# Attention, group norm and ternary feed-forward in one kernel: the inverse softmax sums of two heads travel through DRAM instead of over TensorE

## What is computed

```
s1 = q1 @ k1^T * scale + causal mask ; a1 = softmax(s1)      # 16 heads, q1, q2, k1, k2 of 32 columns each, with rope
s2 = q2 @ k2^T * scale + causal mask ; a2 = softmax(s2)
out = (a1 - lam * a2) @ v                                    # v has 64 columns, 4 key-value heads
out = (out - mean(T, 64)) * rsqrt(var(T, 64) + eps) * gn_w + gn_b       # over time and width of one head
x = layernorm(x + (out * KEEP) @ Wo)
x = layernorm(x + down(silu(up(x)) * gate(x)))               # weights quantised to -1, 0, 1 times a scale
```

## Time and profile before

| what | value |
|---|---|
| median of 3 runs | 2199.38 us (2192.79 to 2201.3) |
| profiled execution: its own time | 2201.01 us |
| profiled execution: span from first to last instruction | 2196.6 us |
| granted TensorE clock, mean over the span | 0.992 |
| PE busy, share of the span | 97% |
| DVE busy | 77% |
| ACT busy | 66% |
| POOL busy | 54% |
| bytes moved by DMA | 263.85 MB, mean 120 GB/s |

### The profile page before, as it was taken

The page is one execution under the profiler, slowest core; times in us unless marked ns, Lnnn a source line. Parts: engine busy times, 40 slices in busy tenths (PEclk is TensorE's granted clock), DMA queues, the critical chain, the costliest instruction groups (busy, mean ns, idle before and its releaser), DMA issues.

```text
span 2196.6 us, 41181 instructions
## 1 busy us (share of the span) xinstructions
PE 2125.6 (97%) x13314; PEld 1367.8 (62%) x13314; DVE 1688.4 (77%) x3701; ACT 1458.0 (66%) x3450; POOL 1194.4 (54%) x1919
## 2 busy tenths in 40 slices
PE   8999999999999999999999999999999999999998
PEld 4666666666665766666666666666666666654443
DVE  4888888889888887788887888878778788853333
ACT  0777777667776777777667777777677687742232
POOL 0577666677655655555654655655455555531232
PEclk9999999999999999999999999999999999999999
DMA  7666576757655512212462322342552212114000
GB/s 252 200 210 219 195 216 198 238 180 221 189 163 149 163 51 61 92 50 62 145 153 79 97 68 84 96 125 73 154 116 54 73 40 87 49 49 110 6 20 19
DMA packets 291217, 263.85 MB, mean 120 GB/s; under 512 B 65088, under 2 KB 233152, under 8 KB 288960
## 3 DMA queue, kind: packets, MB, share of 16 engines
q1 hardware_dynamic: 279808, 228.65, 35.6%
q10 hardware_dynamic: 11200, 32.58, 4.6%
HBM read 181.48 MB, written 71.30 MB: 115 GB/s over the span
## 4 chain that ended last, share of the span: by engine, by line
PE 77%; DVE 8%; POOL 5%; issue 5%; ACT 4%; DMA 1%; ACTq 0%; DVEq 0%; SPq 0%; POOLq 0%
PE PS L1171 18%; PE PS L1120 11%; PE PS L1101 10%; PE PS L1082 10%; PE PS L1140 9%; PE PS L1161 9%; PE PS L1180 8%; PE PS L1147 2%; DVE e_long L1458 2%; POOL linv L1383 2%; ACT dt_long L1222 1%; ACT e_long L1232 1%; POOL coef L1384 1%; PE PS L1086 1%; DVE e_long L1524 1%
## 5 line engine op out<-in xcount | busy, mean ns | idle before, releaser
L1383 POOL TENSOR_TENSOR linv<-lsum,powers 128x2 f32<-128x2 f32 x512 | 405.7, 792 | 415.5 <-ACT e_long L1232 340.2
L1232 ACT ACTIVATE e_long<-e_long,nmax 128x768 f32<-128x768 f32 (+3 forms) x512 | 505.2, 987 | 159.5 <-DVE nmax L1458 156.8
L1458 DVE CUSTOM_DVE_ANT_0 e_long<-PS,mask_b 128x768 f32<-128x768 f32 (+3 forms) x512 | 516.8, 1019 | 82.1 <-PE PS L1101 61.0
L1101 PE MATMUL PS<-kstk,qstk 128*128 128x384 f32 (+5 forms) x1536 | 479.0, 416 | 19.6 <-DVE nmax L1458 9.5
L1101 PEld LDWEIGHTS PS<-kstk,qstk 128*128 128x128 f32 x1536 | 269.7, 191 | 144.5 <-issue 83.8
L1222 ACT ACTIVATE dt_long<-PS 128x512 f32<-128x512 f32 (+3 forms) x544 | 258.4, 514 | 136.5 <-PE PS L1082 126.5
L1524 DVE SCALAR_TENSOR_TENSOR e_long<-e_long,coef 128x1024 f32<-128x1024 f32 (+3 forms) x256 | 276.6, 1080 | 68.4 <-POOL coef L1384 68.0
L1232 ACT ACTIVATE e_short<-e_short,nmax 128x384 f32<-128x384 f32 (+3 forms) x512 | 283.1, 557 | 20.1 <-DVE nmax L1458 19.4
L1396 POOL TENSOR_TENSOR hid<-th,hid 128x512 f16<-128x512 f32 x128 | 148.2, 1160 | 248.8 <-ACT hid L1272 129.6
L1384 POOL TENSOR_SCALAR coef<-lsum,linv,neglam 128x1 f32<-128x1 f32 x512 | 233.2, 456 | 53.4
L1082 PE MATMUL PS<-ident,e_long 128*128 128x128 f32 x1664 | 239.6, 276 | 13.9 <-DVE nmax L1458 7.1
(11 more groups left out here) (117 smaller groups left out, 3114.9 us busy)
## 6 DMA issues: line engine op xcount, KB each, us to landing
qstk<-dq SPq DMA_DIRECT2D x512, 128.0 KB, 2.9
dq<-hl SPq DMA_DIRECT2D x25, 1024.0 KB, 5.1
wr<-in_w_proj ACTq DMA_DIRECT2D x48, 512.0 KB, 5.1
kstk<-dk SPq DMA_DIRECT2D x64, 256.0 KB, 5.2
da<-ra SPq DMA_DIRECT2D x32, 512.0 KB, 3.3
at_sb<-da SPq DMA_DIRECT2D x32, 512.0 KB, 4.3
wt<-in_w_up SPq DMA_DIRECT2D x16, 512.0 KB, 6.0
wt<-in_w_gate SPq DMA_DIRECT2D x16, 512.0 KB, 5.5
```

The costliest lines, as they stand in the source:

```text
L1101: last = nc.tensor.matmul(slot[:, h, :], qstk[:, duo % 4, 2 * r + m, :].bitcast(F32R), kstk[:, g % 2, m, h * w:(h + 1) * w].bitcast(F32R), ...
L1232: nc.scalar.activation(e, e, ACT.Exp, bias=nmax[:, u % 8:u % 8 + 1], scale=-1.0, accum_out=lsum[:, n % 4, m:m + 1]).then_inc(s_exp, 1)
L1383: link(nc.gpsimd.tensor_tensor(linv[:, a % 8, :], lsum[:, a % 4, :], mone, ALU.pow))
L1458: nc.vector.tensor_tensor_reduce(out, slot, mask, -1.0, -NEG, ALU.add, ALU.min, nmax[:, u % 8:u % 8 + 1]).then_inc(s_negmax, 1)
```

## The change

The way of the inverses is another one. `spread`, turn and copy are gone: POOL no longer writes `wide`, PE no longer turns it, ACT evicts only key blocks, and `r_short` and the last block of `dt_long` are gone. Instead SP issues, for each duo, one store of the two columns of `linv` (128 partitions, two numbers of 4 bytes each) to two rows of 128 numbers in DRAM (`dinv`), waits for its landing, and issues two loads, each of which reads one row into 64 partitions of a new tile `inverses` (four duos deep). `product` waits for the rows and multiplies by them. The eviction of a head step no longer waits for the product that read the rows out of the same tile. `factor` waits, from head step 8 on, for the landing of the store that last read its column of `linv`. In the planner the new DMAs get costs (0.5 and 0.9 us on SP) and a landing time of 3.0 us each, evictions and turns get the costs of their key blocks alone, and `PACE` goes from 3.75 to 3.6.

```diff
@@ -63,14 +63,9 @@
-def in_line(duo):
-    return STEPS[heads_of(duo)[0]].t != 3
-    return (STEPS[n].t + STEPS[n].r) // 4 + 1
+    return STEPS[n].t // 4 + 1
@@ -206,7 +201,7 @@
-LANDS = {"load q": 4.5, "load k": 7.5, "load v": 6.0, "store v": 7.0, "store rotated": 8, "store a": 4.5, "load a": 6.5,
+LANDS = {"store inverses": 3.0, "load inverses": 3.0, "load q": 4.5, "load k": 7.5, "load v": 6.0, "store v": 7.0, "store rotated": 8, "store a": 4.5, "load a": 6.5,
@@ -216,8 +211,7 @@
-    t, r = STEPS[n].t, STEPS[n].r
-    return min(4, t + 1 + r - 4 * half), min(4, t + 1 - 4 * half)
+    return min(4, STEPS[n].t + 1 - 4 * half)
@@ -233,7 +227,7 @@
-        return 0.109 * blocks_of(a, b)[0] + 0.02
+        return 0.109 * blocks_of(a, b) + 0.02
@@ -241,10 +235,7 @@
-        blocks, keys = blocks_of(a, b)
-        if in_line(STEPS[a].duo) or blocks == keys:
-            return 0.06 + 0.107 * blocks
-        return 0.22 + (0.06 + 0.107 * keys if keys else 0)
+        return 0.06 + 0.107 * blocks_of(a, b)
@@ -253,11 +244,11 @@
-        return 1.4 if STEPS[a].r else 1.15
+        return 1.15
-            "load q": 1.0, "load k": 1.9, "load first": 0.5, "load x1": 0.5, "load wo": 0.48, "load a": 0.5, "store v": 0.45,
+            "store inverses": 0.5, "load inverses": 0.9, "load q": 1.0, "load k": 1.9, "load first": 0.5, "load x1": 0.5, "load wo": 0.48, "load a": 0.5, "store v": 0.45,
@@ -296,10 +287,6 @@
-            if STEPS[back].r:
-                out.append(ITEM("product", STEPS[back].duo))
-        if STEPS[a].r and not in_line(STEPS[a].duo) and STEPS[a].duo >= 8:
-            out.append(ITEM("product", STEPS[a].duo - 8))
@@ -371,7 +358,7 @@
-        out = [ITEM("values", run_of(a))]
+        out = [ITEM("values", run_of(a)), ITEM("load inverses", a)]
@@ -390,9 +377,12 @@
-        if STEPS[a].r and STEPS[a].duo >= 2:
-            second = heads_of(STEPS[a].duo - 2)[1]
-            out.append(ITEM("turn", second, turns(second) - 1))
+        if a >= 8:
+            out.append(ITEM("store inverses", STEPS[a - 8].duo))
+    elif what == "store inverses":
+        out = [ITEM("factor", heads_of(a)[1])] + [ITEM("load inverses", a - 4)] * (a >= 4)
+    elif what == "load inverses":
+        out = [ITEM("store inverses", a)] + [ITEM("product", a - 4)] * (a >= 4)
@@ -476,6 +466,7 @@
+           [ITEM("store inverses", duo) for duo in range(DUOS)], [ITEM("load inverses", duo) for duo in range(DUOS)],
@@ -487,9 +478,9 @@
-         "sum": -1.5, "ternary": -1.5, "side": -1.0, "rsqrt": 1.0, "product": 0.5, "load q": 2.0, "store rotated": 3.0}
+         "sum": -1.5, "ternary": -1.5, "side": -1.0, "rsqrt": 1.0, "product": 0.5, "load q": 2.0, "store inverses": 1.5, "load inverses": 1.5, "store rotated": 3.0}
-PACE = 3.75
+PACE = 3.6
@@ -697,6 +688,7 @@
+    dinv = nc.dram_tensor("dinv", (DUOS, 2, P), F32, kind="Internal").ap()
@@ -745,10 +737,9 @@
-        dt_long = [sb(f"dt_long{r}", [P, NT + r, P]) for r in range(2)]
+        dt_long = [sb(f"dt_long{r}", [P, NT, P]) for r in range(2)]
-        r_short = sb("r_short", [P, P])
-        wide = sb("wide", [P, 2, 2, 64])
+        inverses = sb("inverses", [P, 4, P])
@@ -845,7 +836,8 @@
-        s_wide = sem("s_wide")
+        s_inv = [sem(f"s_inv{k}") for k in range(4)]
+        s_rows = [sem(f"s_rows{k}") for k in range(4)]
@@ -870,6 +862,9 @@
+        def inverses_stored(eng, duo):
+            eng.wait_ge(s_inv[duo % 4], 16 * (duo // 4 + 1))
@@ -958,6 +953,21 @@
+            def store_inverses(duo):
+                second = heads_of(duo)[1]
+                sp.wait_ge(s_coef, second + 1)
+                sp.dma_start(dinv[duo].rearrange("r q -> q r"), linv[:, (second - 2) % 8:second % 8 + 1:2, 0],
+                             allow_slow_non_contiguous=True)\
+                    .then_inc(s_inv[duo % 4], 16)
+            def load_inverses(duo):
+                inverses_stored(sp, duo)
+                if duo >= 4:
+                    multiplied(sp, duo - 4)
+                for r in range(2):
+                    sp.dma_start(inverses[64 * r:64 * r + 64, duo % 4, :], dinv[duo, r:r + 1, :].broadcast_to((64, P)))\
+                        .then_inc(s_rows[duo % 4], 16)
@@ -1044,6 +1054,10 @@
+                elif what == "store inverses":
+                    store_inverses(a)
+                elif what == "load inverses":
+                    load_inverses(a)
@@ -1076,15 +1090,9 @@
-                blocks, keys = blocks_of(n, half)
-                for k in range(keys):
+                for k in range(blocks_of(n, half)):
-                if blocks > keys:
-                    duo = STEPS[n].duo
-                    pe.wait_ge(s_wide, duo + 1)
-                    last = nc.tensor.transpose(F[bank][:, keys * P:blocks * P],
-                                               wide[:, duo % 2, :, :].rearrange("p r d -> p (r d)"), ident[:, :])
@@ -1206,24 +1214,14 @@
-                blocks, keys = blocks_of(n, half)
-                duo = STEPS[n].duo
+                blocks = blocks_of(n, half)
-                    if STEPS[back].r:
-                        multiplied(act, STEPS[back].duo)
-                if half == 0 and STEPS[n].r and not in_line(duo) and duo >= 8:
-                    multiplied(act, duo - 8)
-                here = blocks if in_line(duo) else keys
-                if here > 0:
-                    copied = nc.scalar.activation(
-                        dt_of(n)[:, 4 * half:4 * half + here, :].rearrange("p k q -> p (k q)"), F[bank][:, 0:here * P], ACT.Copy)
-                if here < blocks:
-                    copied = nc.scalar.activation(r_short[:, :], F[bank][:, here * P:blocks * P], ACT.Copy)
-                copied.then_inc(s_ffree[bank], 1)
+                nc.scalar.activation(dt_of(n)[:, 4 * half:4 * half + blocks, :].rearrange("p k q -> p (k q)"),
+                                     F[bank][:, 0:blocks * P], ACT.Copy).then_inc(s_ffree[bank], 1)
@@ -1378,17 +1376,12 @@
-                    duo = STEPS[a].duo
+                    if a >= 8:
+                        inverses_stored(pool, STEPS[a - 8].duo)
-                    if STEPS[a].r:
-                        if duo >= 2:
-                            second = heads_of(duo - 2)[1]
-                            pool.wait_ge(s_tb, TURN[second, turns(second) - 1] + 1)
-                        nc.gpsimd.tensor_copy(wide[:, duo % 2, :, :], linv[:, (a - 2) % 8:a % 8 + 1:2, 0:1]
-                                              .broadcast_to((P, 2, 64))).then_inc(s_wide, 1)
@@ -1542,12 +1535,13 @@
-                    rows = dt_of(heads_of(a)[1])[:, t + 1, :] if in_line(a) else r_short[:, :]
+                    dve.wait_ge(s_rows[a % 4], 32 * (a // 4 + 1))
-                    nc.vector.tensor_tensor(ra[:, chunk % 2, t * P:(t + 1) * P], F[bank][:, a % 2 * P:a % 2 * P + P], rows,
+                    nc.vector.tensor_tensor(ra[:, chunk % 2, t * P:(t + 1) * P], F[bank][:, a % 2 * P:a % 2 * P + P],
+                                            inverses[:, a % 4, :],
```

## The result

The changed kernel takes 3056.81 us (median of 4 runs, 3038.47 to 3063.27) where the kernel before takes 2197.53 us: 1.390 times the time of before, 95% interval 1.383 to 1.397. The profiled execution took 3038.47 us, with a span of 3036.7 us. The forecast was 2173.4 us, with a range up to 2200.

A forecast was written before the change was run, and what follows sets the result against it. PE was taken to bound all three stages, with DVE close behind in the first. Terms -28.9 - 2 - 2 + 2 + 5 = -26 us gave 2175 us against the profiled execution, 2173.4 us for the median; range 2150 to 2200.

The forecast's parts named there:

- What bounds the kernel: Whole run: PE sets the time in all three stages, busy 97% of the span; taking columns from it shortens the run.
- Turns, POOL, ACT and pace: Attention: fewer turned blocks -28.9 us, lone turns -2, POOL's copies -2, ACT's evictions nothing, closer pace +5.
- The new way of the rows: Store, landing and loads ahead of DVE's product: path 5.3 to 6.8 us, hidden in usual windows of 9.3 us; charged 2 us.
- The term for late rows: DVE's product: rows come first usually, the shortest windows lose 1 us; 2 us charged in the sum.
- What waits behind them: SP's queue and POOL's `factor`: waits for the store's landing cost nothing while it stays below some 10 us.
- The DMA engines: Small pieces on the DMA engines: at most 276 us of packets, 13% of the span; longer landings, but no bound.
- the rows come late: Rival at DVE's wait in `product`: decides from a store landing after 5.8 us; 64 us reach PE, 2237 us; chance 0.12.

The follow-up runs named there:

- e1_no_rows: Changed kernel without store and loads of the inverses, product by a constant tile of ones, division by the sums left out: 2173.97 us, 0.990 of before.
- e1b_no_rows_375: As e1_no_rows, with the old PACE of 3.75 instead of 3.6: 2184.82 us.
- e6_spread: Changed kernel with the store's pieces 512 bytes apart in DRAM, loads reading a fixed input row, division by the sums left out: 2240.76 us.
- e11_64: As e6_spread, with the pieces 64 bytes apart in DRAM: 2238.84 us.
- e12_256: As e6_spread, with the pieces 256 bytes apart in DRAM: 2235.15 us.
- e4_no_wait: Changed kernel with all DMAs and SP's waits, but the product multiplies by a constant without waiting for rows, division left out: 2661.17 us.
- e8_stores_only: As e1_no_rows, with the 256 stores to DRAM kept, pieces side by side, no loads of inverses: 2311.32 us.
- e13_stores_spread: As e8_stores_only, with the pieces 512 bytes apart in DRAM: 2163.07 us.

## Why the prediction was wrong

**What bounds the kernel** held. PE was the bound, and what takes its columns away shortens the run (e1_no_rows).

**Turns, POOL, ACT and pace** held as a sum and not in their parts. The terms come to -28.9 - 2 - 2 + 5 = -28 us; e1_no_rows measured 2196.6 - 2174.0 = 22.6 us of gain. Without the change of pace the first three (32.9 us together) brought 2196.5 - 2184.8 = 11.7 us. The pace was put at +5, as a price; it is a gain of 5.1 us in the kernel before and of 10.9 us with the turns gone. So two misses in opposite ways made the sum good, and part of that is luck. The argument behind it was sound: at the old pace the fills do run out ahead of the last output projection (the hole in e1b_no_rows_375), for about half of the 20 us that it allowed.

**The new way of the rows** is the step that failed. "The nearest rows are those of 128 KB in 256 pieces of 512 bytes" put the store at 2.1 to 3.3 us. The count of pieces was the wrong likeness; side by side in DRAM they take 9.8 us, and 2.3 when spread (e6_spread, e11_64, e12_256). None of the rows had pieces of a few bytes side by side in DRAM. The term for late rows stood at 2 us in the sum. The path became at least 9.8 + 0.6 + 3.5 = 13.9 us, with 3.5 the landing of the loads in the kernel after, where 9.3 us were there to hide it.

**What waits behind them** failed with it, and more. The text said that both waits cost nothing while the landing stays below some 10 us, on the ground that q is loaded three duos early. The landing was just below, and these waits stood at nothing in the sum. With the loads they cost 350 us above the kernel that has the stores alone (e4_no_wait against e8_stores_only), and q came late. A wait at the head of a queue holds back not one transfer but all that follow, the next duo's store among them, so the landings of one wait and the next add up: 180 waits, 1210.1 us. The slack of one load of q is the wrong measure for that. POOL's wait in `factor` did cost next to nothing (8.9 us in two waits in e8_stores_only).

**The DMA engines.** The estimate was 276 us of packets at most. When spread, the 65536 pieces took 818.6 - 783.5 = 35 us of the 16 engines and no time that can be measured (e13_stores_spread, 2163 us). Side by side they took 318 us, the other packets' slowness with them, and 148 us of the kernel's time (e8_stores_only against e13_stores_spread), which no step had.

**The rival** "the rows come late" named the right place, DVE's wait in `product`, and the right point, 5.8 us for the store. Its price of 64 us rested on a lateness of 1 us for each even duo. It was 6.0 us in 119 products; PE's waits grew with it, and its clock fell. It had 0.12. The rule of the Trainium skill on transposing by an access pattern, in "VectorE: DVE Perf Modes", section "The three transpose paths", spoke for this rival. Its factor of 19 is against the crossbar's way and for a large innermost stride of the destination; no run here has the crossbar's way, and the close store took about 4 times as long as the spread one. The rule of the Trainium skill on a strided last dimension, in "DMA: Bandwidth & Descriptors", section "Rules for kernel authors", advises against the spread store as much as against the close one; the spread one landed after 2.3 us, and here the measurement decides.

## What to carry to other kernels

In this kernel a landing went by where the pieces fell more than by their number: before a small transposing store is hidden behind anything, its landing has to be measured alone. A DMA queue that waits for its own store pays that latency each time it waits (here 180 times), so count store-then-load turns in the queue, and put the true landing into the planner (here 486 us). And try the gain without its cost first: a kernel that leaves the new transfers out tells what there is to win (here 1%), and so how little latency it can pay for.

## What the runs showed of the hardware

Stores of 256 pieces of 4 bytes into DRAM land after 9.8 us (median) when the pieces are side by side, and after 2.3 us when they are 64, 256 or 512 bytes apart. Stores of 128 such pieces side by side land after 8.2 us in DRAM and after 2.3 us in SBUF. In the kernel with close stores other transfers of the same core land later than in the one with spread stores: 128 KB loads after 5.5 us instead of 2.9 (e8_stores_only, e13_stores_spread). Two such stores issued 0.65 us apart (at 1351.38 and 1352.04 us of the kernel after) landed at 1360.0 and 1360.2 us, so they overlap; one is not queued behind the other. In the kernel after PE's clock spent 755 us at 1.2 GHz in 101 stretches, in the kernel before 41 us in 10; PE had stood still for more than 1 us 140 and 15 times.
